# First layer of a four-layer kernel: scores as one 64-row product per head, projections of eight heads laid out through HBM

## Chip, cores and metric

The kernel runs on one core of one Trainium2 chip. The metric is the device time of the whole program in microseconds (us), the median of the runs. Engines are named as in the profile: PE (TensorE matmul), PEld (its weight load), DVE (VectorE), ACT (ScalarE), POOL (GpSimd), SP (SyncE, which here only issues DMAs).

## Reference

Four layers work one after the other on x (8 batches x 256 channels x 512 positions), with ctx of the same shape. The change touches the first one alone:

```python
q = Wq @ x + bq ; k = Wk @ ctx + bk ; v = Wv @ ctx + bv      # per batch, 256 x 512
# 16 heads of 16 channels each
attn = softmax((q * scale)^T k, masked keys -> -inf)         # per head 512 x 512
mean = attn @ v ; ex2 = attn @ (v * v)                       # per head 512 x 16
std  = sqrt(relu(ex2 - mean * mean))
out  = (instance_norm(x, mask) * std + mean) * mask
```

Layers 2 (a recurrent block), 3 (two cross attentions and an MLP) and 4 (a non-local block) are the same code before and after.

## The kernel before

**Precision.** PE multiplies float32 operands of the kind fp32r in one pass, at less than full precision. So every operand A is kept as a high part (A rounded) and a low part (A minus high), and a product is high x high + high x low + low x high: three passes that accumulate in the same PSUM bank.

**Heads and groups.** `layer0` handles the 16 heads of a batch in four groups (`G0`) of four heads (`HG`); there are 8 batches, so 32 groups. A head has 16 channels, but gets 32 rows of the 128 partitions: 16 for the channels, row `ROW_MASK` for the additive mask of the keys (the queries hold 4.0 there), row `ROW_MAX` for the negated maximum of the query (the keys hold 1.0 there). The tiles QH, QL (queries, high and low) and KH, KL (keys) have 128 partitions = 4 heads x 32 rows, a slot for each of the four groups, and 512 columns. `project_queries` (6 passes of 512 columns) and `project_keys` (6 passes and one with MSELR that adds the mask row) make them for one group. ACT evicts the PSUM bank as the high part (L545, L550), DVE then evicts the same bank as the low part (L684, L689).

**A group** is 8 steps (`NT`; n = 0 to 7), each for one pair of heads and one quarter of the 512 keys. In a step PE does, in this order: `scores` (L417: three passes, each for two heads in two different 32-row parts of the array, into two of the four banks BT), `maxima` (L394: one high x high pass for the group two ahead, into the two banks BM), `weighted` of the step before (L431: exponentials times values and squares, for two heads), and then what else that step carries. ACT takes the exponential of the score banks (L582), DVE the maximum over the maxima banks (L695). Further work in a step: n = 1 `turn_maxima` (a transpose, which DVE casts to NMT), n = 2 and 6 `turn_pair` (four transposes of the result, of which DVE takes the moments), n = 3 `project_queries` and n = 4 `project_keys` for the group three ahead, in group 3 n = 5 and 7 `values` of the next batch, in group 2 n = 7 `statistics`.

**What sets the order.** It is written out by hand: each engine has its own program, and semaphores join them. `maxima(n)` waits until DVE has read `maxima(n-1)` (one pair of banks BM), `scores(n)` waits for the exponential of n - 2, `weighted(n)` for that of n, `weighted` of a group's first step also for the squares that ACT writes (`square_values`, L567). SP places the four turned maxima of a group as one row each by DMA (`place_maxima`, L177), a group before they are used; scores of a group wait for them. ACT's square roots in group 0 (`roots`) need other tables: a load before them and one behind. Ahead of the first group (the prologue) PE projects three groups and DVE takes the maxima of two groups, 16 reductions.

Of the kernel before, what the change touches and what calls it, by code (L numbers as in the profile page):

```python
# [5 lines left out]

# [14 lines left out]
G0 = 4  # L21
HG = H0 // G0
CG = HG * D0
ROW_MASK, ROW_MAX = D0, D0 + 1
# [3 lines left out]
NEG = -1e30  # L28
# [21 lines left out]
def layer0(nc, x, xT, ctx, mask_row, mask_col, wqk, qkb, aug, wv, bv, mask_sel, ident_in, x1T):  # L50
# [5 lines left out]
    with ExitStack() as stack:  # L56
# [17 lines left out]
        WH = sb("wh", [P, G0, LC, 2, P], F32R)  # L74
        WL = sb("wl", [P, G0, LC, 2, P], F32R)
        WVH = sb("wvh", [P, LC, L], F32R)
        WVL = sb("wvl", [P, LC, L], F32R)
        QKB = sb("qkb", [P, 2, G0])
        AUG = sb("aug", [P, 2, G0])
        BVB = sb("bvb", [P, L])  # L80
        MSEL = sb("msel", [P, P])
        MSELR = sb("mselr", [P, P], F32R)
# [16 lines left out]
        QH = sb("qh", [P, G0, E], F32R)  # L99
        QL = sb("ql", [P, G0, E], F32R)  # L100
        KH = sb("kh", [P, G0, E], F32R)
        KL = sb("kl", [P, G0, E], F32R)
# [15 lines left out]
        WQK = EX[:, 0:2, :, :].rearrange("p n a (b c d) -> p (n a) b c d", b=LC, c=2)  # L118
# [3 lines left out]

        consts_in, inputs_in, stats_x_in, memset_done, inputs_read, mask_read, stats_read = [sem(n) for n in ("consts_in", "inputs_in", "stats_x_in", "memset_done", "inputs_read", "mask_read", "stats_read")]
# [23 lines left out]
        def head_rows(p, a):  # L147

            h = 2 * p + a
            return slice(32 * h, 32 * h + 32)  # L150

        @block.sync
        def _(sp):
# [17 lines left out]
            def place_maxima(b, g):  # L171
# [4 lines left out]
                for h in range(HG):  # L176
                    sp.dma_start(QH[32 * h + ROW_MAX:32 * h + ROW_MAX + 1, g, :].bitcast(F32),  # L177
                                 NMT[h * EC:(h + 1) * EC, g % 2, :].bitcast(F32)).then_inc(max_in, 16)
# [3 lines left out]
            for dst, src in ((QKB[:, :, :], qkb), (AUG[:, :, :], aug), (MSEL[:, :], mask_sel), (WV, wv), (BVB[:, :], bv),  # L182
                             (ID[:, :], ident_in)):
                sp.dma_start(dst, src).then_inc(consts_in, 16)
            load_statistics(0)
            place_maxima(0, 0)
            load_inputs(1)
            place_maxima(0, 1)
            with sp.Fori(0, B - 2) as b:
# [3031 lines left out]
```

## Time and profile before

| | us |
|---|---|
| median of 3 runs | 4405.9 (4405.7 to 4408.11) |
| span of the profiled execution | 4404.7 |
| PE busy over the span | 4165.1 (95%) |
| DVE busy | 2982.4 (68%) |
| ACT busy | 1964.2 (45%) |
| POOL busy | 1591.1 (36%) |
| mean granted TensorE clock | 0.978 |
| HBM read, written | 220.27 MB, 15.73 MB |

The profiled execution stands 1.2 us below the median. The chain of waits that the page prints covers the last layer alone; for the first layer the timeline is what tells. The first layer runs from 0 to about 829 us.

### The profile page before, as it was taken

How to read it: one execution, taken by the hardware profiler on the slowest of the kernel's cores; microseconds unless marked ns; L12 is line 12 of the kernel's file. 1: busy time of each engine (PE TensorE's matmuls, PEld its weight loads, DVE VectorE, ACT ScalarE, POOL GpSimd, SP SyncE). 2: the span in 40 equal slices, each digit the busy share in tenths (PEclk: the TensorE clock that was granted, in tenths of full speed). 3: DMA queues.
4: the chain of work that ended last, by engine and by line, in shares of the span. 5: the costliest groups of instructions: out<-in, count | busy, mean ns of one | idle time of the engine just before them, and what ended most of it. 6: DMA issues, size and time to landing. Idle time of an engine off the chain costs nothing. (4 is left out here: it accounts for less than half of the span.)

```text
span 4404.7 us, 70578 instructions
## 1 busy us (share of the span) xinstructions
PE 4165.1 (95%) x22060; PEld 3143.8 (71%) x22060; DVE 2982.4 (68%) x6501; ACT 1964.2 (45%) x3814; POOL 1591.1 (36%) x1094
## 2 busy tenths in 40 slices
PE   7999999778999997799999999999999999999999
PEld 3444444356777775588887797887887877988866
DVE  5666666268888887475775775767766757757743
ACT  2555555322333331355553455553555543555522
POOL 1223233145566563133234323234332234332230
PEclk7999999889999999899999999999999999999999
DMA  1000000300000000222112322222222122231122
GB/s 40 26 20 30 20 20 11 125 5 11 15 15 15 16 10 15 90 63 83 58 60 74 103 63 73 64 72 72 92 65 71 58 70 99 63 96 56 54 78 98
DMA packets 128413, 239.26 MB, mean 54 GB/s; under 512 B 16933, under 2 KB 40101, under 8 KB 126897
## 3 DMA queue, kind: packets, MB, share of 16 engines
q1 hardware_dynamic: 126544, 232.46, 16.5%
q0 software_dynamic: 1008, 3.67, 0.2%
q8 instruction: 123, 2.02, 0.2%
q14 instruction: 114, 0.93, 0.1%
q10 hardware_dynamic: 624, 0.18, 0.0%
HBM read 220.27 MB, written 15.73 MB: 54 GB/s over the span
## 5 line engine op out<-in xcount | busy, mean ns | idle before, releaser
L2105 POOL TENSOR_TENSOR c_wl<-c_wr,c_wh 128x512 fp32r<-128x512 f32 (+1 forms) x576 | 822.0, 1439 | 1646.0 <-ACT c_wh L2472 1388.7
L2573 ACT ACTIVATE c_pr<-c_ps,c_nms 128x257 f32<-128x257 f32 x512 | 244.2, 477 | 485.1 <-DVE c_nms L2795 483.1
L582 ACT ACTIVATE a_ex<-a_ps 128x1024 f32<-128x1024 f32 x256 | 261.1, 1023 | 259.7 <-PE a_ps L417 259.7
L1629 DVE TENSOR_TENSOR_SCAN b_sb<-b_wt,b_s,b_ps 128x256 f32<-128x256 f32 x512 | 361.6, 735 | 15.6 <-PE b_ps L1082 3.2
L695 DVE TENSOR_REDUCE a_nm<-a_ps 128x2 f32<-128x1024 f32 x256 | 311.4, 1221 | 80.5 <-PE a_ps L394 80.3
L2472 ACT ACTIVATE c_wh<-c_wr 128x512 fp32r<-128x512 f32 (+1 forms) x464 | 315.3, 687 | 45.4 <-PE c_ps L2192 41.6
L1580 POOL TENSOR_TENSOR b_sb<-b_sb,b_rt 128x1024 f32<-128x1024 f32 x128 | 277.9, 2178 | 156.5 <-DVE b_sb L1629 113.9
L2190 PE MATMUL c_ps<-c_hh,c_wh 128*128 128x512 f32 x768 | 309.1, 402 | 12.9 <-DVE c_hl L2679 12.6
L2190 PE MATMUL c_ps<-c_gh,c_wh 128*128 128x512 f32 x768 | 307.7, 401 | 5.6 <-DVE c_gl L2857 2.9
L2192 PE MATMUL c_ps<-c_hh,c_wl 128*128 128x512 f32 x768 | 304.4, 396 | 0.0
L2191 PE MATMUL c_ps<-c_hl,c_wh 128*128 128x512 f32 x768 | 303.8, 396 | 0.0
L2190 PE MATMUL c_ps<-c_wh,c_cth 128*128 128x256 f32 x1024 | 303.5, 296 | 0.0
L2192 PE MATMUL c_ps<-c_gh,c_wl 128*128 128x512 f32 x768 | 303.3, 395 | 0.0
L2191 PE MATMUL c_ps<-c_gl,c_wh 128*128 128x512 f32 x768 | 302.9, 394 | 0.0
L2192 PE MATMUL c_ps<-c_wh,c_ctl 128*128 128x256 f32 x1024 | 288.3, 282 | 0.0
L2191 PE MATMUL c_ps<-c_wl,c_cth 128*128 128x256 f32 x1024 | 287.7, 281 | 0.0
L431 PE MATMUL a_ps<-a_ex,a_vf 128*64 128x512 f32 x1024 | 278.9, 623 | 8.9 <-ACT a_ex L582 7.9
L2793 DVE TENSOR_REDUCE c_nm<-c_ps 128x1 f32<-128x257 f32 x512 | 214.9, 420 | 69.5 <-PE c_ps L2192 69.3
L1094 PE MATMUL b_ps<-b_xf,b_w 128*128 128x256 f32 x1056 | 243.6, 384 | 12.1 <-DVEq L1688 10.1
L1094 PEld LDWEIGHTS b_ps<-b_xf,b_w 128*128 128x128 f32 x1056 | 199.9, 192 | 46.3 <-issue 14.7
L2837 DVE TENSOR_TENSOR c_gl<-c_g,c_gh 128x512 fp32r<-128x512 f32 x128 | 89.2, 702 | 206.1 <-ACT c_gh L2555 206.1
L2789 DVE TENSOR_SCALAR c_pr<-c_pr,c_rs 128x257 f32<-128x257 f32 x512 | 196.1, 383 | 40.3 <-issue 1.0
(379 smaller groups left out, 10578.6 us busy)
## 6 DMA issues: line engine op xcount, KB each, us to landing
c_wr<-in_downs SPq DMA_DIRECT2D x192, 256.0 KB, 2.7
c_wr<-in_wv SPq DMA_DIRECT2D x64, 512.0 KB, 3.9
c_wr<-in_wk SPq DMA_DIRECT2D x128, 256.0 KB, 2.9
c_wr<-in_wq SPq DMA_DIRECT2D x128, 256.0 KB, 2.6
c_wr<-in_fc SPq DMA_DIRECT2D x64, 256.0 KB, 2.8
b_w<-in_w SPq DMA_DIRECT2D x8, 1024.0 KB, 14.7
a_x<-in_x SPq DMA_DIRECT2D x8, 512.0 KB, 3.9
a_ctx<-in_ctx SPq DMA_DIRECT2D x8, 512.0 KB, 4.4
```

The costliest lines, as they stand in the source:

```text
L431: mm = pe.matmul(ps[64 * a:64 * a + VCOLS, BO, :], VF[:, k, g * HG + 2 * p + a, :], EX[:, n % 4, a, :], start=(k == 0), stop=(k == EC - 1) ...
L582: act.activation(EX[:, n % 4, :, :], ps[:, BT + 2 * (n % 2):BT + 2 * (n % 2) + 2, :], ACT.Exp).then_inc(ex_ready, 1)
L695: dve.tensor_reduce(NM[:, s, :].rearrange("p (h c) -> p h c", h=HG)[:, 2 * p:2 * p + 2, c:c + 1], ps[:, bank:bank + 2, :], AX.X, ALU.max, ...
L1094: mm = pe.matmul(half(bank, o), W[:, w, k, o * P:(o + 1) * P], src[:, k, :], start=(k == 0), stop=(k == EC - 1), skip_group_check=True)
L1580: pool.tensor_tensor(SB[:, quad % RING, :, :, 0:L], SB[:, quad % RING, :, :, 0:L], RT[:, third(b, q // 8)].unsqueeze(1).broadcast_to([P, 2 ...
L1629: mm = dve.tensor_tensor_scan(SB[:, quad % RING, pr % 2, e, 1:L + 1], WT[:, third(b, i), e, :], half(spread_bank(pair), e), S0[:, b % 2, 2 ...
L2105: pool.tensor_tensor(piece(WL, slot), piece(WR, slot), piece(WH, slot), ALU.subtract).then_inc(piece_cut[slot], 1)
L2190: pe.matmul(out, sh, mh, start=start, stop=False, skip_group_check=True)
L2191: pe.matmul(out, sh, ml, start=False, stop=False, skip_group_check=True)
L2192: return pe.matmul(out, sl, mh, start=False, stop=stop, skip_group_check=True)
L2472: act.activation(piece(WH, slot), piece(WR, slot), ACT.Copy).then_inc(piece_high[slot], 1)
L2573: act.activation(PR[:, i, 0:L + 1], ps[:, BS + 1 - i % 2, 0:L + 1], ACT.Exp, bias=NMS[:, i:i + 1], scale=float(K2) ** -0.5, accum_out=RS[: ...
```

## The change

- A head has 64 rows: 16 with the high part, 16 that pair high with low, 16 that pair low with high, the mask row (48, `ROW_MASK`) and the row of the maximum (49, `ROW_MAX`); rows 50 to 63 hold zeros. Queries hold high, high, low, and keys hold high, low, high. So one pass is the whole score. `scores` has one pass in place of three; `maxima` stays one pass, now with all 64 rows.
- The projections yield eight heads of 16 rows without gaps (an "oct", `OCT` = 2 for each batch) in place of four heads of 32. There are two of each kind in a batch in place of four, in groups 0 and 2, and for the next batch. The pass with MSELR is gone; the mask row is written by DMA.
- The 64-row layout is made by DMA: SP writes the high and low parts to a tensor `strips` in HBM (7 writes for an oct: `write_queries`, `write_keys`) and reads them back into the tiles QP and KP (4 reads for a group: `place_strips`), once the scores that read the slot are done. Constant rows are written to HBM at the start by four DMAs of ACT.
- The rounding of ctx to its high part (`cut_c` on ACT) moves from group 1, n = 0 to group 0, n = 0, ahead of the squares of the values; that of x (`cut_x`) to group 3, n = 5. `mask_rows` and `count_valid` on DVE move from groups 0 and 1 to group 3.
- In the prologue the four projections of batch 0 go to four banks in one go, then the values, then the maxima of two groups.

```diff
-ROW_MASK, ROW_MAX = D0, D0 + 1
+ROWS = 64
+ROW_MASK, ROW_MAX = 3 * D0, 3 * D0 + 1
+OCT = 2
...
+            def write_queries(b, o):
+
+                for g in (2 * o, 2 * o + 1):
+                    sp.wait_ge(strips_in[g], b * N_STRIPS + AHEAD)
+                    sp.sem_inc(passed, 1)
+                sp.wait_ge(qh_ready, b * OCT + o + 1 + AHEAD)
+                sp.sem_inc(passed, 1)
+                sp.dma_start(scratch_rows(0, o, 0, D0), QH[:, :].bitcast(F32)).then_inc(scratch_in[o], 16)
+                sp.dma_start(scratch_rows(0, o, D0, D0), QH[:, :].bitcast(F32)).then_inc(scratch_in[o], 16)
+                sp.wait_ge(ql_ready, b * OCT + o + 1 + AHEAD)
+                sp.sem_inc(passed, 1)
+                sp.dma_start(scratch_rows(0, o, 2 * D0, D0), QL[:, :].bitcast(F32)).then_inc(scratch_in[o], 16)
...
+            def place_strips(b, g):
+
+                sp.wait_ge(scratch_in[g // 2], (b + 1) * N_SCRATCH + AHEAD)
+                sp.sem_inc(passed, 1)
+                sp.wait_ge(t_ps, (b * G0 + g - G0 + 1) * NT + AHEAD)
+                sp.sem_inc(passed, 1)
+                for s, tile in ((0, QP), (1, KP)):
+                    for a in range(2):
+                        heads = strips[s, g // 2, :, HG * (g % 2) + a:HG * (g % 2) + HG:2, :]
+                        sp.dma_start(tile[head_rows(a), g, :, :].bitcast(F32), heads).then_inc(strips_in[g], 16)
...
             with sp.Fori(0, B - 2) as b:
-                place_maxima(b, 2)
+                place_strips(b + 1, 1)
                 place_maxima(b, 3)
                 load_statistics(b + 1)
+                load_inputs(b + 2)
+                write_queries(b + 1, 1)
+                write_keys(b + 1, 1)
+                place_strips(b + 1, 2)
                 place_maxima(b + 1, 0)
-                load_inputs(b + 2)
+                place_strips(b + 1, 3)
                 place_maxima(b + 1, 1)
+                write_queries(b + 2, 0)
+                write_keys(b + 2, 0)
+                place_strips(b + 2, 0)
+                place_maxima(b + 1, 2)
...
-                pe.matmul(ps[:, BX, :], MSELR[:, :], MBRR[:, :], start=False, stop=True).then_inc(k_ps, 1)
...
-                for i, (keys, queries) in enumerate(((KH, QH), (KH, QL), (KL, QH))):
-                    for a in range(2):
-                        rows = head_rows(p, a)
-                        mm = pe.matmul(ps[:, BT + 2 * (n % 2) + a, :], keys[rows, g, cols], queries[rows, g, :], start=(i == 0), stop=(i == 2))
+                for a in range(2):
+                    rows = head_rows(a)
+                    mm = pe.matmul(ps[:, BT + 2 * (n % 2) + a, :], KP[rows, g, p, cols], QP[rows, g, p, :], start=True, stop=True)
...
-                    if left > 2 and n == QUERIES_AT:
+                    if projected and n == QUERIES_AT:
...
-                        project_queries(*after(b, g, 3))
-                    if left > 2 and n == KEYS_AT:
-                        project_keys(*after(b, g, 3))
+                        project_queries(b + 1, g // 2)
+                    if projected and n == KEYS_AT:
+                        project_keys(b + 1, g // 2)
...
-                    if g == 1 and left > 2 and n == 0:
+                    if g == 0 and more and n == 0:
                         cut_c(b + 1)
```

PE in step n = 4 of a group that projects, before (a_qh, a_ql, a_kh and a_kl are the tiles of queries and keys, a_ch and a_cl ctx, a_ps PSUM):

```order
L417 MATMUL a_ps<-a_qh,a_kh 128x512 [waits a_ex_ready]
L417 MATMUL a_ps<-a_qh,a_kh 128x512
L417 MATMUL a_ps<-a_ql,a_kh 128x512 x2
L417 MATMUL a_ps<-a_qh,a_kl 128x512 x2
L391 REGISTER_ALU
L394 MATMUL a_ps<-a_kh,a_qh 128x512 [waits a_m_read]
L394 MATMUL a_ps<-a_kh,a_qh 128x512
L431 MATMUL a_ps<-a_ex,a_vf 64x512 [waits a_ex_ready]
L431 MATMUL a_ps<-a_ex,a_vf 64x512
L352 REGISTER_ALU [waits a_mask_ready,a_c_low]
L355 MATMUL a_ps<-a_ch,a_wh 128x512 [waits a_ql_ready,a_qh_ready]
```

And the same step after (a_qp and a_kp are the 64-row tiles):

```order
L481 MATMUL a_ps<-a_qp,a_kp 128x512 [waits a_ex_ready]
L481 MATMUL a_ps<-a_qp,a_kp 128x512
L461 MATMUL a_ps<-a_kp,a_qp 128x512 [waits a_m_read]
L461 MATMUL a_ps<-a_kp,a_qp 128x512
L495 MATMUL a_ps<-a_ex,a_vf 64x512 [waits a_ex_ready]
L495 MATMUL a_ps<-a_ex,a_vf 64x512
L423 MATMUL a_ps<-a_ch,a_wh 128x512 [waits a_ql_ready,a_qh_ready]
```

Four of the eight row-tiled matmuls are gone, and the wait for a_m_read (DVE has read the maxima before) stands two passes nearer to the step's start.

ACT at the start of group 0 in the loop before (a_ex the exponentials, a_ot the result of a pair, a_vf values and squares):

```order
L582 ACTIVATE a_ex<-a_ps 128x1024 [waits a_w_ps]
L572 ISA
L573 REGISTER_ALU [waits a_w_ps]
L574 ACTIVATE a_ot<-a_ps 128x512 [waits a_tr_ps]
L565 ISA
L566 ISA [waits a_vs_ready]
L567 ACTIVATE a_vf<-a_vs 128x4x4x16 [waits a_w_ps]
```

And after:

```order
L652 ACTIVATE a_ex<-a_ps 128x1024 [waits a_w_ps]
L642 ISA
L643 REGISTER_ALU [waits a_w_ps]
L644 ACTIVATE a_ot<-a_ps 128x512 [waits a_tr_ps]
L630 ACTIVATE a_ch<-a_ctx 128x1024 [waits a_v_ps,a_k_ps,a_inputs_in]
L636 ISA [waits a_vs_ready]
L637 ACTIVATE a_vf<-a_vs 128x4x4x16 [waits a_w_ps]
```

The rounding of ctx (128x1024) now stands ahead of the squares.

SP from step 3 of group 2 to step 1 of group 3 in the loop after (before, SP issued in this place the turned maxima and the loads of inputs, nothing else):

```order
L197 DMA strips<-a_qh 8x16x512
L200 DMA strips<-a_ql 8x16x512 [waits a_ql_ready]
L208 DMA strips<-a_kh 8x16x512 [waits a_mask_ready,a_kh_ready]
L209 DMA strips<-a_kh 8x16x512
L210 DMA strips<-a_mbrr 8x512
L213 DMA strips<-a_kl 8x16x512 [waits a_kl_ready]
L219 ISA [waits a_scratch_in1]
L224 DMA a_qp<-strips 64x2x512 [waits a_t_ps]
L224 DMA a_qp<-strips 64x2x512
L224 DMA a_kp<-strips 64x2x512 x2
L183 REGISTER_ALU
L187 DMA a_qp<-a_nmT 1x4x128 [waits a_nmT_sb]
```

The placing of the maxima now stands behind reads that wait for the end of a group's scores (a_t_ps).

## Rows read from the trace of the kernel before

**Rows 1.** Windows: busy us of PE, PEld, DVE, ACT, POOL; clock, DMA share, GB/s

```profile
0.00:60.00 60.00, 31.37 (x96) 19.72 (x96) 33.79 (x39) 8.88 (x11) 5.34 (x11) 0.73 0.22 73
258.00:350.00 92.00, 90.73 (x490) 44.26 (x488) 57.10 (x77) 49.86 (x59) 29.41 (x29) 1.00 0.08 24
```

**Rows 2.** Timeline, one plain step (start us, us, engine, line)

```profile
298.95 0.49 PE L417 MATMUL a_ps<-a_qh,a_kh 32*128 32x512 f32 x2
...
299.52 0.39 PE L417 MATMUL a_ps<-a_qh,a_kl 32*128 32x512 f32 x2
...
299.75 0.39 PE L394 MATMUL a_ps<-a_kh,a_qh 32*128 32x512 f32 x2
...
299.96 1.02 ACT L582 ACTIVATE a_ex<-a_ps 128x1024 f32<-128x1024 f32 x1 [1.69 <-PE a_ps L417]
...
300.08 1.08 PE L431 MATMUL a_ps<-a_ex,a_vf 128*64 128x512 f32 x4
300.19 1.23 DVE L695 TENSOR_REDUCE a_nm<-a_ps 128x2 f32<-128x1024 f32 x1 [0.42 <-PE a_ps L394]
...
301.09 0.50 PE L417 MATMUL a_ps<-a_qh,a_kh 32*128 32x512 f32 x2
```

**Rows 3.** Timeline of the prologue and the first scores

```profile
27.95 0.96 PE L394 MATMUL a_ps<-a_kh,a_qh 32*128 32x512 f32 x6
...
29.44 3.48 DVE L695 TENSOR_REDUCE a_nm<-a_ps 128x2 f32<-128x1024 f32 x3
...
31.84 0.80 PE L394 MATMUL a_ps<-a_kh,a_qh 32*128 32x512 f32 x2 [0.63 <-DVE a_nm L695]
...
60.27 0.79 PE L417 MATMUL a_ps<-a_qh,a_kh 32*128 32x512 f32 x2 [2.89 <-DVE a_nm L695]
```

**Rows 4.** Timeline, projections in steps 3 and 4 of a group

```profile
265.48 0.50 PE L341 MATMUL a_ps<-a_xh,a_wh 128*128 128x512 f32 x1
...
267.06 0.50 PE L417 MATMUL a_ps<-a_qh,a_kh 32*128 32x512 f32 x2
...
269.21 0.50 PE L355 MATMUL a_ps<-a_ch,a_wh 128*128 128x512 f32 x1
...
271.04 0.50 PE L417 MATMUL a_ps<-a_qh,a_kh 32*128 32x512 f32 x2
...
271.15 0.69 ACT L550 ACTIVATE a_kh<-a_ps,a_qkb 128x512 fp32r<-128x512 f32 x1 [1.15 <-PE a_ps L358]
...
271.87 0.75 DVE L689 SCALAR_TENSOR_TENSOR a_kl<-a_ps,a_qkb,a_kh 128x512 fp32r<-128x512 f32 x1 [2.09 <-ACT a_kh L550]
```

**Rows 5.** Timeline, ACT's extra work in groups 0 and 1, and who waits

```profile
258.74 0.41 ACT L567 ACTIVATE a_vf<-a_vs 128x256 f32<-128x256 f32 x1
...
259.39 0.65 PE L431 MATMUL a_ps<-a_ex,a_vf 128*64 128x512 f32 x2
...
273.10 1.28 ACT L612 ACT_TABLE_LOAD   x1
...
277.16 1.94 ACT L582 ACTIVATE a_ex<-a_ps 128x1024 f32<-128x1024 f32 x2
...
278.24 1.08 PE L431 MATMUL a_ps<-a_ex,a_vf 128*64 128x512 f32 x4 [1.13 <-ACT a_ex L582]
...
282.16 1.05 ACT L560 ACTIVATE a_ch<-a_ctx 128x1024 fp32r<-128x1024 f32 x1
```

**Rows 6.** Timeline, DVE's extra work beside the reductions

```profile
279.82 0.95 DVE L799 RECIPROCAL a_st<-a_st 128x128 f32<-128x128 f32 x1
...
329.02 0.41 DVE L748 TENSOR_TENSOR a_st<-a_st 128x256 f32<-128x256 f32 x1
...
330.24 0.15 DVE L753 RECIPROCAL a_rn<-a_nv 128x1 f32<-128x1 f32 x1
```

**Rows 7.** DMA issues: size, us to landing; and SP's issues of one group

```profile
c_wr<-in_downs SPq DMA_DIRECT2D x192, 256.0 KB, 2.7
...
261.19 2.49 SPq L177 DMA_DIRECT2D a_qh<-a_nmT  x4
```

More of the change, by code:

```diff
@@ L7 @@
+import itertools
 from contextlib import ExitStack
@@ L279, in group_0 @@
                 copy_values(b, 1)
+                if more:
+                    cut_c(b + 1)
                 if prior is not None:
@@ L443, in before, with group @@
                 return (b, g - 1) if g > 0 else (b - 1, G0 - 1)
-            def group(b, g, left=3, first=False):
+            def group(b, g, left=3, first=False, more=True):
                 it = b * G0 + g
+                projected = more and g % 2 == 0
                 for n in range(NT):
@@ L574, in take_pair, with group @@
                 act.activation(OT[:, p, :], ps[:, BO, :], ACT.Copy).then_inc(ot_ready, 1)
-            def group(b, g, left=3, prior=None, first=False, more=True):
+            def group(b, g, prior=None, first=False, more=True, further=True):
                 it = b * G0 + g
@@ L591, in group @@
                         square_values(b, g + 1)
[L592 to L593 removed]
+                    if more and g % 2 == 0 and n == QUERIES_AT:
+                        queries(b + 1, g // 2)
                     if n == 4:
                         take_pair(b, g, 0)
[L596 to L597 removed]
+                    if more and g % 2 == 0 and n == KEYS_AT:
+                        keys(b + 1, g // 2)
                     if g == 2 and n == 5:
@@ L620, in _ @@
             act.wait_ge(weights_split, 2 + AHEAD)
-            for g in range(3):
-                queries(0, g)
-                keys(0, g)
+            queries(0, 0, BT)
+            keys(0, 0, BT + 1)
+            queries(0, 1, BT + 2)
+            keys(0, 1, BT + 3)
             square_values(0, 0)
+            cut_x(1)
             group(0, 0, first=True)
@@ L753, in spread_of_x, with group @@
                 dve.reciprocal(RN[:, :], NV[:, :])
-            def group(b, g, left=3, prior=None, first=False, more=True):
+            def group(b, g, left=3, prior=None, first=False, more=True, further=True):
                 for n in range(NT):
@@ L767, in group @@
                             take_moments(b - 1, G0 - 1, 1)
-                    if left > 2 and n == QUERIES_AT:
-                        queries(*after(b, g, 3))
-                    if left > 2 and n == KEYS_AT:
-                        keys(*after(b, g, 3))
+                    if more and g % 2 == 0 and n == QUERIES_AT:
+                        queries(b + 1, g // 2)
+                    if more and g % 2 == 0 and n == KEYS_AT:
+                        keys(b + 1, g // 2)
                     if left and g == G0 - 1 and n == VALUES_AT[0]:
@@ L830, in _ @@
             mask_rows(0, 1)
+            queries(0, 0, BT)
+            keys(0, 0, BT + 1)
             count_valid(0)
```

311 lines of the change are left out of this document (165 added, 146 removed).

## The prediction

> **What bounds the kernel now.** I read the windows first. In the middle of the first layer PE is busy 90.7 of 92 us at full clock, while DVE has 57.1, ACT 49.9 and POOL 29.4 [rows 1]. The change touches only this layer, which ends near 829 of 4404.7 us; the rest is left as it is.
>
> Next comes the timeline of a plain step [rows 2]. PE starts the first score pass at 298.95, the third at 299.52, the maxima pass at 299.75, the weighted product at 300.08, and the next step's scores at 301.09. So the step takes 2.14 us, without a gap. A pass costs 0.23 (299.52 to 299.75); a first pass after another shape costs 0.10 more (0.57 for two). ACT's exponential starts 0.44 behind the last score pass and takes 1.02. DVE's maximum starts 0.44 behind the maxima pass and takes 1.23. Both have room in 2.14 us. PE is the bound, so PE time removed is time won, until the next engine is met.
>
> **What is removed.**
> - Scores: 256 steps (32 groups x 8) lose two passes of 0.23 each. The saving is 256 x 0.46 = 117.8 us. The plain step becomes 1.68.
> - Projections: queries take 265.48 to 267.06 = 1.58, keys 269.21 to 271.04 = 1.83 with the mask pass [rows 4]. 29 of the 32 groups are projected inside steps, 29 x 3.41 = 98.9. After, there are 7 batches x 2, each 1.58 + 1.60, together 44.5. The saving is 54.4.
> - Prologue: scores start at 60.27 and the first maxima pass at 27.95, 32.3 us for 16 reductions. These alone need 16 x 1.16 = 18.6 (3.48 for three, [rows 3]); the rest is the third projection and the values, which now lie ahead of them. The first maxima must now wait for the layout: two projections to about 17 us, evictions of 0.69 and 0.75 [rows 4], seven writes at 0.62 per issue (2.49 for four) and 2.7 to land, four reads at the same prices [rows 7]. That comes to about 28 us, where the first maxima are today. I take 28 + 18.6 + 0.6 = 47, a saving of 13.
>
> Together 117.8 + 54.4 + 13 = 185 us.
>
> **What is given back**, where a shorter PE step uncovers another engine.
> - DVE's floor. There is one pair of maxima banks. The maxima pass, 0.44 to the reduction, 1.23 for it, and 0.12 until PE goes on (the second reduction ends at 29.44 + 2 x 1.14 = 31.72, PE starts at 31.84 [rows 3]) make 1.79 per step. Against 1.68 this costs 0.1 in the some 9 steps of a batch without PE extras: 7 us in all.
> - Behind the projection of keys. ACT starts 0.11 behind the step's first pass and takes 0.69; DVE's low part starts 0.03 later and takes 0.75; only then comes the reduction of 1.23, and 0.12 [rows 4, 2]. So the next maxima pass cannot start before 2.95 us into the step. Before, PE reached it at 2.14 + 0.80 = 2.94; now it is there at 2.0. Cost 0.95, in group 2 of seven batches and group 0 of the first: 8 x 0.95 = 7.6. Queries cost nothing: the keys' projection covers their eviction.
> - ACT in group 0. `cut_c` (1.05, [rows 5]) now stands ahead of the squares, for which the weighted product of step 1 waits. Before, the squares ended at 259.15 and PE went on at 259.39, a stall of 0.2 us. Now they come 1.05 - 0.46 = 0.6 later and PE is 2 x 0.46 = 0.9 earlier: 1.5 us more, in six batches, 9 us.
> - The square roots of group 0: the exponential of step 5, a table load at 273.10, two roots, a load, the exponential of step 6 at 277.16 and PE at 278.24 [rows 5], which waited 1.13. This chain hangs on step 5's start and is not shortened, so the three last steps stay at 8.0 us (before 8.2) and their saved 1.4 is lost but for 0.2: 1.2 x 7 = 8.5.
> - DVE's extra work. A reciprocal of 0.95 stands behind group 1's first reduction (2.3 us with it, against a step of 1.79), and 1.37 (329.02 to 330.39) ahead of the second in group 3 [rows 6]. Similar pieces lie at the seam of groups 1 and 2. I estimate 2 us per batch, 14 in all.
> - HBM layout, SP and its queue: nothing. An oct's strips are projected at steps 3 and 4 of a group. They are read at the end of that group or of a later one, and used a group after that, 15 us or more later. A read needs 4 x 0.62 + 2.7 = 5.2 [rows 7]. SP issues some 51 DMAs per batch of 80 us, 32 us. The turned maxima come behind the reads in SP's program but are ready only at step 1, when the reads (2.5 us of issue) are nearly out, and have over 10 us. Should a group be shorter than this path, all of the excess would show.
>
> Sum: 7 + 7.6 + 9 + 8.5 + 14 = 46. Net gain 185 - 46 = 139. Against the profiled span this gives 4404.7 - 139 = 4265.7; the median is 1.2 above the span, so 4267. A batch takes some 96 us now (60 to 829 us in eight) and should take about 81.
>
> **Two unknown prices.** No row shows a 64-row pass. It is bounded by the 32-row pair at 0.23, where both heads run at once, and by the two heads one after the other, 0.46. I take 0.23, the nearest row: it too has two heads in separate rows of the array.
>
> The Trainium skill ("TensorEngine Tiling (Array Packing)", Tiling Modes) lists two tiles of 64 rows x 128 columns that work in parallel, which is the first of these prices. The trace shows it for 32 rows only. By its sentence on mode switches, which drain the engine, nothing changes, since there are two switches per step before and after.
>
> The other is the write to HBM in 8 x 16 x 512 form, between the 2.7 us of a 256 KB load and twice that. In the loop either is hidden. In the prologue the double would take back some 5 of the 13 us.
>
> A rule that speaks against the layout: the Trainium skill ("DMA: Bandwidth & Descriptors", Why a DMA increments its semaphore by 16 and not by 1) says that a copy runs on the largest number of DMA engines up to 16 that divides the slowest dimension of both sides. That is 8 for the 8 x 16 x 512 side, half the engines. By this the doubled price would hold, and the time would be 4272 instead of 4267.
>
> **The rivals.**
> 1. The 64-row heads do not run at once. Each of the two row-tiled passes then costs 0.46, and the plain step stays at 2.14. The score saving is gone, and of the give-backs only ACT's squares stay: 54.4 + 13 - 9 = 58, so 4347. For it: no row has this shape. Against it: 32-row pairs do. Chance 0.06.
> 2. The give-backs are mostly hidden, for instance because the work overlaps more finely than my step by step count: up to 4405.9 - 185 = 4221. Against it: each is a chain read from rows. Chance 0.06 for below 4240.
> 3. Slower: the layout path becomes the bound. `maxima` for a group two ahead wait for strips that SP may read only once the old slot's scores are done. In group 0 the write and the two round trips then set the pace of every group. It decides once the reads land later than a group (15 to 16 us) after their issue, and the kernel is slower from about 16 + 139 / 28 = 21 us on. A landing of 25 us would give 28 x 9 - 139 = 113 us more, 4519. For it: SP is in order and strips move 7.3 MB per batch, some 90 GB/s on top of 24 [rows 1]. Against it: a 256 KB load lands in 2.7. Chance 0.03.
> 4. The clock. It was 0.73 in the first 60 us, where PE was busy 31.4 us and waited for DVE, and 1.00 where it was busy throughout [rows 1]. After, PE is busy some 73 of 80 us, with gaps of up to 1.5 us. If a tenth of the eight batches (65 us) ran at 1.2 in place of 2.4 GHz, it would cost 0.9 x 65 = 58 us: 4325. Chance 0.05.
>
> **The numbers.** My case has 0.80, with 4250 to 4290 as its own range. The range for all reaches down to 4235, halfway to the case without give-backs, and up to 4320, towards the clock and to late strips of a few us. That leaves out rival 1 (0.06), rival 3 (0.03), half of rivals 2 and 4, and some 0.04 beyond. A difference under 0.2% (9 us) cannot be told from none. Faster by more than that: 0.80 + 0.06 + 0.06 + 0.04 = 0.96, cut to 0.95. Same 0.01, slower 0.04.
>
> **What would show it.** The score pair should stand 0.34 ahead of the maxima pass, with plain steps of 1.7 to 1.8 us and DVE the releaser of the maxima pass. The step behind a keys' projection should be near 3.2 us, `weighted` in step 1 of group 0 should wait for ACT, and first scores should start near 47 us. PE waiting for DMA within a batch would prove me wrong, as would a score pair of 0.46, or a granted clock below 0.95 between 150 and 600 us.

## The result: 4275.6 us, and the profile after

The changed kernel takes 4275.63 us (median of 4 runs, 4275.28 to 4276.14), the kernel before 4406.14 us in the same session (4 runs, 4405.7 to 4408.11). The ratio is 0.970, with an interval of 0.969 to 0.972: faster by 130.5 us, where 139 were forecast. The profiled execution spans 4274.3 us, 130.4 less than before.

The windows of the trace come first. Columns are as in [rows 1]: length, busy us of PE, PEld, DVE, ACT and POOL, granted clock, DMA share, GB/s.

```profile
0.00:28.00 28.00, 8.18 (x24) 6.20 (x24) 8.20 (x12) 5.30 (x6) 4.59 (x9) 0.94 0.49 169
28.00:46.00 18.00, 8.36 (x41) 5.98 (x41) 12.87 (x14) 1.68 (x3) 0.40 (x1) 0.69 0.71 202
46.00:60.00 14.00, 6.65 (x21) 2.94 (x23) 9.42 (x9) 1.06 (x1) 2.69 (x2) 0.50 1.04 263
150.00:600.00 450.00, 420.38 (x1981) 170.52 (x1980) 307.63 (x413) 265.73 (x311) 168.77 (x174) 1.00 0.41 120
```

In the loop (last row) PE is busy 93% of the time at full clock, where [rows 1] has 99% (of another stretch). What is missing is the give-back: PE now waits for other engines. The DMA share has gone from 0.08 to 0.41. The first three rows are the prologue, and the DMA engines are full in the third.

A plain step and two that are held show how PE's time is spent. These are lines of the timeline of the changed kernel (start, length, engine, line, and in brackets how long the engine sat idle and what ended it). L481 is the score pair, L461 the maxima pass, L495 the weighted product, L763 DVE's reduction, L652 the exponential. The rows from 314.07 answer to [rows 2], and with the key eviction at 314.90 to [rows 4].

```profile
314.07 0.50 PE L481 MATMUL a_ps<-a_qp,a_kp 64*128 64x512 f32 x2
...
314.41 0.39 PE L461 MATMUL a_ps<-a_kp,a_qp 64*128 64x512 f32 x2
...
314.90 0.75 DVE L757 SCALAR_TENSOR_TENSOR a_kl<-a_ps,a_qkb,a_kh 128x512 fp32r<-128x512 f32 x1 [1.41 <-ACT a_kh L617]
...
315.57 1.22 DVE L763 TENSOR_REDUCE a_nm<-a_ps 128x2 f32<-128x1024 f32 x1
...
315.75 0.49 PE L481 MATMUL a_ps<-a_qp,a_kp 64*128 64x512 f32 x2
...
316.84 0.51 PE L461 MATMUL a_ps<-a_kp,a_qp 64*128 64x512 f32 x2 [0.60 <-DVE a_nm L763]
...
318.87 0.50 PE L481 MATMUL a_ps<-a_qp,a_kp 64*128 64x512 f32 x2
...
320.94 1.08 PE L495 MATMUL a_ps<-a_ex,a_vf 128*64 128x512 f32 x4 [1.33 <-ACT a_ex L652]
...
321.95 0.50 PE L481 MATMUL a_ps<-a_qp,a_kp 64*128 64x512 f32 x2
```

From 314.07 to 315.75 is one step of PE's own work: 1.68 us, as forecast. The score pair stands 0.34 ahead of the maxima pass, so a 64-row pair costs what a 32-row pair does. The next step lasts 3.12 (to 318.87), because DVE evicted `a_kl` before it reduced. The last lasts 3.08, because the exponential stands behind two square roots and two table loads. Counted in this way, a batch in the middle takes 21.87 + 15.42 + 23.77 + 19.51 = 80.57 us (groups 0 to 3), where it was 95.8 and some 81 were forecast.

Who made PE wait between 80 and 600 us, by the view of waits (us in total, times, longest):

```profile
PE a_ps L461 <- DVE a_nm L763: 15.7, 32, 0.9
PE a_ps L495 <- ACT a_vf L637: 8.4, 6, 1.4
PE a_ps L495 <- ACT a_ex L652: 8.0, 6, 1.3
```

These three are the give-backs that the prediction lists, and there is none for a DMA. The view counts idle time alone: the step at 315.75 lasts 3.12 us, where a step of this kind with three passes (below) takes 2.72 and should take 2.26 with one. That is 0.86 more, and the view shows a wait of 0.60. So a give-back is better read from the length of steps than from this view.

The prologue is where the forecast failed. The timeline of the changed kernel there, which answers to [rows 3] (L196 to L213 are SP's writes to the strips, L224 its reads):

```profile
16.43 0.76 SPq L196 DMA_DIRECT2D strips<-a_qh  x1
...
20.40 1.68 SPq L210 DMA_DIRECT2D strips<-a_mbrr  x1
...
22.20 1.06 SPq L213 DMA_DIRECT2D strips<-a_kl  x1
...
28.04 0.69 ACT L613 ACTIVATE a_qh<-a_ps,a_qkb 128x512 fp32r<-128x512 f32 x1 [9.31 <-DMA strips<-a_kl]
28.17 1.32 SPq L224 DMA_DIRECT2D a_qp<-strips  x2
...
35.95 0.97 PE L461 MATMUL a_ps<-a_kp,a_qp 64*128 64x512 f32 x6
...
48.83 1.65 PE L461 MATMUL a_ps<-a_kp,a_qp 64*128 64x512 f32 x6 [2.46 <-DMA a_kp<-strips]
...
59.34 0.79 PE L481 MATMUL a_ps<-a_qp,a_kp 64*128 64x512 f32 x2 [3.07 <-DVE a_nm L763]
```

SP issues the seven writes from 16.43 to 23.26, they have landed at 28.04, the first maxima start at 35.95 and the first scores at 59.34. The forecast had 47, and before it was 60.27. So the 13 us of the prologue came out as 0.9, and that is 12 us less than forecast.

Where the rest of the 130.4 lies is seen at PE's first matmul of layer 2, which starts at 833.00 us before and at 707.43 after. So the first layer is 125.6 us shorter, 0.9 of it in the prologue and 124.7 behind it, where 126 were forecast. The other 4.8 us lie in layers 2 to 4, whose code is the same. From that matmul to the end, the kernel before and its variant with one pass take 3571.7 and 3572.6 us, the changed kernel and its nine variants 3564.1 to 3567.9. No run asks for the cause, and it stays open.

### The profile page after: what moved, and what is told of

It reads as the page before. It is cut to its first block and busy times, and to the rows that moved or that the text cites. A ratio compares the mean times of both kernels' runs of the same rounds, so it can differ in the third digit from the quotient of the medians.

```text
span 4274.3 us, 68335 instructions
## 1 busy us (share of the span) xinstructions
PE 3998.9 (94%) x20812; PEld 3013.6 (71%) x20812; DVE 2939.8 (69%) x6467; ACT 1935.0 (45%) x3782; POOL 1592.7 (37%) x1094
## 5 line engine op out<-in xcount | busy, mean ns | idle before, releaser
L652 ACT ACTIVATE a_ex<-a_ps 128x1024 f32<-128x1024 f32 x256 | 260.9, 1022 | 212.8 <-PE a_ps L481 212.8
L763 DVE TENSOR_REDUCE a_nm<-a_ps 128x2 f32<-128x1024 f32 x256 | 311.5, 1221 | 60.7 <-PE a_ps L461 59.1
L495 PE MATMUL a_ps<-a_ex,a_vf 128*64 128x512 f32 x1024 | 278.1, 621 | 20.5 <-ACT a_ex L652 9.8
L1165 PE MATMUL b_ps<-b_xf,b_w 128*128 128x256 f32 x1056 | 243.6, 384 | 12.1 <-DVEq L1759 10.1
```

Of the source, the lines that this page charges most:

```text
L495: mm = pe.matmul(ps[64 * a:64 * a + VCOLS, BO, :], VF[:, k, g * HG + 2 * p + a, :], EX[:, n % 4, a, :], start=(k == 0), stop=(k == EC - 1) ...
L652: act.activation(EX[:, n % 4, :, :], ps[:, BT + 2 * (n % 2):BT + 2 * (n % 2) + 2, :], ACT.Exp).then_inc(ex_ready, 1)
L763: dve.tensor_reduce(NM[:, s, :].rearrange("p (h c) -> p h c", h=HG)[:, 2 * p:2 * p + 2, c:c + 1], ps[:, bank:bank + 2, :], AX.X, ALU.max, ...
L1165: mm = pe.matmul(half(bank, o), W[:, w, k, o * P:(o + 1) * P], src[:, k, :], start=(k == 0), stop=(k == EC - 1), skip_group_check=True)
```

## The experiments

Ten kernels were run. The kernel before, timed beside them, had 4406.5 to 4407.2 us.

### Each score pass three times

```diff
-                for a in range(2):
-                    rows = head_rows(a)
-                    mm = pe.matmul(ps[:, BT + 2 * (n % 2) + a, :], KP[rows, g, p, cols], QP[rows, g, p, :], start=True, stop=True)
+                for i in range(3):
+                    for a in range(2):
+                        rows = head_rows(a)
+                        mm = pe.matmul(ps[:, BT + 2 * (n % 2) + a, :], KP[rows, g, p, cols], QP[rows, g, p, :], start=True, stop=True)
```

This kernel is called three_passes further on.

> The changed kernel with each score pass of 64 rows issued three times into the same banks (the result is that of the last pass, so the scores are unchanged): 256 steps get two passes of 0.23 us back. Theory of the prediction (a score pass costs 0.23, and the shorter steps uncovered DVE and ACT at some 43 us in all, which hide again when the steps are long): +118 - 43 = +75, so 4351 us, plain steps of 2.14 us. Rival: nothing was uncovered and the passes are worth their full time: +118, 4393 us. Second rival: the two 64-row heads of a pass do not run at once; then the step grows by 4 x 0.23, over 4450 us.

Measured: 4348.22 us (4346.59 to 4348.85), ratio 0.987 (0.985 to 0.988). Two steps' first rows in its timeline (the triple score passes are L482):

```profile
343.31 0.96 PE L482 MATMUL a_ps<-a_qp,a_kp 64*128 64x512 f32 x6
...
344.11 0.40 PE L461 MATMUL a_ps<-a_kp,a_qp 64*128 64x512 f32 x2
...
345.45 0.96 PE L482 MATMUL a_ps<-a_qp,a_kp 64*128 64x512 f32 x6
```

Three pairs take 0.80 (343.31 to 344.11), one takes 0.34, so a pair costs 0.23; the step is 2.14 again, and the batch 89.55. Two pairs are worth 256 x 0.46 = 117.8 us of PE time, but only 4348.2 - 4275.6 = 72.6 of time. The other 45.2 are what a short step uncovers. The rest of the change is worth 4406.1 - 4348.2 = 58. It holds nothing of the prologue (the first scores of this kernel come at 60.23), some 5 us that lie behind the first layer, and a loss: here too PE waits 1.09 us for the squares behind `cut_c` (at 331.90), and that step takes 3.49 us. Rival 1, two heads one after the other, falls.

### The kernel before with the high by high pass alone

This leaves the two small products out of the scores, and with them the low parts.

```diff
-                for i, (keys, queries) in enumerate(((KH, QH), (KH, QL), (KL, QH))):
-                    for a in range(2):
-                        rows = head_rows(p, a)
-                        mm = pe.matmul(ps[:, BT + 2 * (n % 2) + a, :], keys[rows, g, cols], queries[rows, g, :], start=(i == 0), stop=(i == 2))
+                for a in range(2):
+                    rows = head_rows(p, a)
+                    mm = pe.matmul(ps[:, BT + 2 * (n % 2) + a, :], KH[rows, g, cols], QH[rows, g, :], start=True, stop=True)
```

> The kernel before with the first score pass alone (high x high; the two passes with a low part are left out, so the scores have less precision). It has neither the HBM layout nor fewer projections. Theory: -118 us of passes, and some 60 us given back (0.95 behind each of the 29 projections of keys = 27.5, DVE's floor 7, square roots 8.5, DVE's extra work 14, squares 3): about 4348 us. Rival: the passes alone are the whole gain, and the halved projections brought nothing: about 4276 us.

Measured: 4356.83 us (4349.54 to 4361.08), ratio 0.988 (0.986 to 0.990), 9 above the expectation. Its undisturbed batch takes 21.15 + 19.88 + 23.70 + 22.60 = 87.3 us, 8.5 less than before, and by eight of these the time would be about 4338. What lengthened it by the other 19 us is seen in a row of its timeline and two windows:

```profile
170.33 1.80 PE L430 MATMUL a_ps<-a_ex,a_vf 128*64 128x512 f32 x4 [1.34 <-ACT a_ex L581]
```

```profile
150.00:171.00 21.00, 18.61 (x87) 7.40 (x87) 14.12 (x18) 14.77 (x18) 5.65 (x7) 0.99 0.00 1
171.00:182.00 11.00, 11.00 (x31) 2.94 (x28) 7.12 (x8) 5.94 (x8) 8.34 (x4) 0.50 0.01 3
```

PE waited 1.34 us for the exponential behind the roots, and then ran at 1.2 GHz for 11 us although it was busy throughout. This happened in group 1 of five batches. In the four of them that lie within the loop that group took 23.9 to 26.3 us in place of 19.9. Rival 4 of the prediction is thus real. The changed kernel has the same wait (1.33 at 320.94) and a clock of 1.00 from 150 to 600 us; only in the last batch, behind a wait of 1.82 us at 638.74, did it run at 0.50 from 640 to 642. Why the clock falls behind one such wait and not behind another stays open.

### cut_c behind the squares

```diff
-                    if g == 0 and more and n == 0:
-                        cut_c(b + 1)
...
                     if g == 0 and n == 0 and not first:
                         square_values(b, 0)
+                    if g == 0 and more and n == 0:
+                        cut_c(b + 1)
```

> The changed kernel with cut_c behind square_values at group 0, n = 0 on ACT. Theory: the weighted product of step 1 waits for the squares, which come 1 us earlier; exponential 1 then comes just in time. 6 batches x 1.0 = -6 us: 4269.5 us, and step 1 of group 0 falls from 3.5 to 2.5 us. Rival: the wait only moves to the exponential of step 1 or to the low part of ctx that the projection of keys needs: within 1 us of 4275.6.

Measured: 4270.80 us (4268.22 to 4273.32), ratio 0.969 (0.967 to 0.971). The timeline of this kernel:

```profile
301.96 0.50 PE L481 MATMUL a_ps<-a_qp,a_kp 64*128 64x512 f32 x2
...
302.65 0.41 ACT L637 ACTIVATE a_vf<-a_vs 128x256 f32<-128x256 f32 x1
...
302.96 1.05 ACT L630 ACTIVATE a_ch<-a_ctx 128x1024 fp32r<-128x1024 f32 x1
...
303.30 1.08 PE L495 MATMUL a_ps<-a_ex,a_vf 128*64 128x512 f32 x4 [0.46 <-ACT a_vf L637]
```

PE's wait in step 1 of group 0 falls from 1.40 to 0.46 us and the step from 3.50 to 2.55, in each batch: 0.95 x 6 = 5.7, and 4.8 in the medians.

### The square roots without their tables

The two square roots in the loop are left out (Identity in their place), so the output is not normed as in the reference.

```diff
-                act.activation(ST[:, 3, :], ST[:, 2, :], ACT.Sqrt, bias=EPS[:, 0:1])
+                act.activation(ST[:, 3, :], ST[:, 2, :], ACT.Identity, bias=EPS[:, 0:1])
-                act.activation(VAR[:, :, :], VAR[:, :, :], ACT.Sqrt).then_inc(std_ready, 1)
+                act.activation(VAR[:, :, :], VAR[:, :, :], ACT.Identity).then_inc(std_ready, 1)
```

> The changed kernel with the two square roots that ScalarE takes for the norm in the loop left out (Identity in their place, so the output is another), which leaves out their table loads too. My theory: in each of the 7 batches group 0 has one step in which TensorE waits about 1.4 us because ScalarE's exponentials stand behind the roots and their tables; without it group 0 goes from 21.9 to about 20.5 us, and the time to about 4275.6 - 7 x 1.4 = 4266 us. Rival: ScalarE is late for other reasons by then (squares, cut_x), the wait only moves to the next step, and the time stays within 3 us of 4275.6.

Measured: 4267.51 us (4263.87 to 4270.32), ratio 0.968 (0.967 to 0.970). The wait for `a_ex` is gone. The last step of group 0 takes 1.67 in place of 3.08 and the group 20.46 in place of 21.87, but group 1 takes 15.92 in place of 15.42. So 0.9 us is won in each of six batches. In the last one, which has no projections, group 0 goes from 18.21 to 15.61 and group 1 from 16.38 to 15.94. That makes 6 x 0.9 + 3.0 = 8.4, and the medians differ by 8.1. Some 1.6 of the 3.0 are the fallen clock of the changed kernel's last batch: with the weights in the order of the strips (below) these two groups take 17.51 and 15.52 at full clock. So the roots themselves are worth nearer 7 us, and their term of 1.2 x 7 = 8.5 had the right place and about the right size.

### The keys' eviction one reduction later

```diff
-                    if more and g % 2 == 0 and n == KEYS_AT:
+                    if more and g % 2 == 0 and n == KEYS_AT + 1:
```

> The changed kernel with VectorE's eviction of the low part of the projected keys taken one reduction later (behind the reduction of the step after KEYS_AT). My theory: the step that follows the projection of keys is held by VectorE's maxima standing behind that eviction, so that step goes from 3.1 to about 2.3 us, once in each of groups 0 and 2 of a batch; at about 0.5 us for each of 14 the time is about 4275.6 - 7 = 4269 us. Rival: VectorE's queue is full there, the next maxima are late by the same amount one step on, and the time stays at 4275.6 within 2 us.

Measured: 4272.21 us (4270.66 to 4276.64), ratio 0.969 (0.968 to 0.971), 3.4 less than the changed kernel, between theory and rival. The timeline of this kernel in group 0:

```profile
318.01 0.50 PE L481 MATMUL a_ps<-a_qp,a_kp 64*128 64x512 f32 x2
...
318.26 0.74 DVE L757 SCALAR_TENSOR_TENSOR a_kl<-a_ps,a_qkb,a_kh 128x512 fp32r<-128x512 f32 x1
318.40 0.51 PE L461 MATMUL a_ps<-a_kp,a_qp 64*128 64x512 f32 x2
...
320.43 0.50 PE L481 MATMUL a_ps<-a_qp,a_kp 64*128 64x512 f32 x2
...
323.20 0.65 PE L495 MATMUL a_ps<-a_ex,a_vf 128*64 128x512 f32 x2 [2.05 <-ACT a_ex L652]
```

The held step falls from 3.12 to 2.42 in groups 0 and 2. In group 2 that is kept (23.77 to 23.05 us). In group 0 PE only arrives earlier at ACT's chain of roots and waits 2.05 there in place of 1.33, so the group stays at 21.87. The stall behind the keys is thus paid once a batch, as the prediction counted it (0.95 x 8; measured 0.71 x 8 = 5.7).

The median shows 3.4 of these 5.7. In batches 1, 2, 4 and 5 (counted from 0) of the profiled run, the slowest of the four, the mean granted clock was 0.76 over 7 us around the end of the wait of 2.05 (in batch 1 it was 0.50 from 161 to 164 us), and groups 0 and 1 together took 38.7 to 38.8 us. In batches 3 and 6 it stayed at 1.00, with 37.3. So a longer wait at the roots brings rival 4 back, at about 1.5 us a time.

### Every read of the strips twice

```diff
+        QD = sb("qd", [P, G0, PAIRS, E], F32R)
+        KD = sb("kd", [P, G0, PAIRS, E], F32R)
...
-        N_SCRATCH, N_STRIPS = 7 * 16, 4 * 16
+        N_SCRATCH, N_STRIPS = 7 * 16, 8 * 16
...
+                        sp.dma_start((QD, KD)[s][head_rows(a), g, :, :].bitcast(F32), heads).then_inc(strips_in[g], 16)
```

The unused reads count on the same semaphore, so PE waits for them as well.

> The changed kernel with every read of the laid-out heads from HBM issued a second time into tiles that nothing uses. My theory: in the loop the layout path has room, no engine waits there for a transfer, so the batches stay at 80.6 us; in the prologue the first maxima wait for the reads and their wait grows by 5 to 10 us, the time comes to about 4282 us. Rival (the layout path is near its bound): the reads end after the group that needs them, the batches grow by several us each, and the time passes 4300 us.

Measured: 4296.09 us (4294.69 to 4299.88), ratio 0.975 (0.974 to 0.977), 20.5 more than the changed kernel. A window, and the timeline of its prologue (scores are L484 here, maxima L464):

```profile
150.00:600.00 450.00, 419.98 (x1994) 171.54 (x1990) 305.80 (x409) 265.32 (x311) 175.16 (x177) 1.00 0.66 168
```

```profile
40.79 1.65 PE L464 MATMUL a_ps<-a_kp,a_qp 64*128 64x512 f32 x6 [4.17 <-DMA a_kd<-strips]
...
59.78 1.65 PE L464 MATMUL a_ps<-a_kp,a_qp 64*128 64x512 f32 x6 [8.45 <-DMA a_kd<-strips]
...
80.22 0.80 PE L484 MATMUL a_ps<-a_qp,a_kp 64*128 64x512 f32 x2 [13.00 <-issue]
```

In the loop the DMA share rises to 0.66 and the batches stay at 80.6 to 80.9 us: the layout costs next to nothing there, even at 1.6 times the load on the DMA engines, and rival 3 falls. All of the loss is in the prologue, where the first scores come at 80.22, 20.9 later. The expectation had 5 to 10 for that, at the first maxima. These come 4.8 us later (40.79), the second group's 11.0 (59.78). The last 9.9 us stand ahead of the scores, in a wait of 13.00 for which the profile names no releaser.

### Weights in the order of the strips, so that each write is one dimension of 128

```diff
-            return strips[s, o, first:first + count, :, :].rearrange("r h e -> h r e")
+            return strips[s, o, first:first + count, :, :].rearrange("r h e -> (r h) e")
...
-        return W.reshape(2,128,2,128).transpose(3,0,2,1)
+        return W.reshape(2,8,16,2,128).transpose(0,2,1,3,4).reshape(2,128,2,128).transpose(3,0,2,1)
```

The biases of queries and keys are reordered in the same way.

> The changed kernel with the weight columns ordered (row, head) in place of (head, row), so that the 128 partitions of QH, QL, KH, KL are written to HBM as one dimension of 128 instead of 8 x 16. Theory: the writes ran on half of the DMA engines (DMA share 0.5 while they alone are under way in the prologue), and now run on all: share near 0.9, the first eight heads land near 23 instead of 28 us, first scores near 51 instead of 59.3: -8 us, 4267.5 us; the batches in the loop unchanged at 80.6 us. Rival: SP's issues or the landing time, not the engines, bound the prologue: under 2 us gained.

Measured: 4267.72 us (4266.06 to 4270.72), ratio 0.969 (0.967 to 0.970), 7.9 less than the changed kernel. Its timeline:

```profile
16.38 0.33 SPq L196 DMA_DIRECT2D strips<-a_qh  x1
...
20.23 0.35 SPq L213 DMA_DIRECT2D strips<-a_kl  x1
22.31 0.69 ACT L613 ACTIVATE a_qh<-a_ps,a_qkb 128x512 fp32r<-128x512 f32 x1 [3.55 <-DMA strips<-a_kl]
22.45 1.34 SPq L224 DMA_DIRECT2D a_qp<-strips  x2
...
30.02 0.74 PE L461 MATMUL a_ps<-a_kp,a_qp 64*128 64x512 f32 x4
...
50.38 0.79 PE L481 MATMUL a_ps<-a_qp,a_kp 64*128 64x512 f32 x2 [2.63 <-DVE a_nm L763]
```

The DMA share from 0 to 60 us, in 40 slices of 1.5 us each and in tenths, of this kernel:

```profile
DMA  0799999000058950899999999999999998100000
```

and of the changed kernel, where the 13th to the 18th slice (18 to 27 us) are the writes:

```profile
DMA  0799989000004555540189955558999999999999
```

The same bytes, written as one dimension of 128 rows, take 0.32 to 0.43 us of SP's time each for the first oct in place of 0.57 to 1.06 (the 16 KB mask row, which took the 1.68 above, takes 0.41), use 0.8 to 0.9 of the DMA engines' time in place of 0.5, and have landed 5.7 us earlier (22.31 for 28.04). Of these, 2.7 us are the earlier end of SP's issues (20.58 for 23.26) and 3.0 the shorter time from there to the landing. The first scores are 8.96 us earlier and the time is shorter by 7.9. The groups in the loop take what they took.

### Staging tiles of its own for the second oct

```diff
+        STAGE = [(QH, QL, KH, KL), tuple(sb(n + "1", [P, E], F32R) for n in ("qh", "ql", "kh", "kl"))]
...
-            write_queries(0, 1)
-            write_keys(0, 1)
+            write_queries(0, 1, 1)
+            write_keys(0, 1, 1)
```

ScalarE's and VectorE's evictions of that oct go to the same new tiles and wait for no earlier write.

> The changed kernel with staging tiles of their own (QH, QL, KH, KL) for the second oct of the first batch, so that ScalarE and VectorE evict it without waiting 9.3 us for the first oct's writes to land. My theory: the writes themselves, on half of the DMA engines, set the first scores; SyncE still reads the first oct behind its writes and writes the second oct behind those reads, so the first scores stay at about 59.3 us and the time at 4275.6 within 3 us. Rival: the shared staging tile is the cause of the late prologue; then the first scores come about 9 us earlier and the time to about 4266 us.

Measured: 4275.43 us (4272.78 to 4277.12), ratio 0.970 (0.969 to 0.972), the first scores at 59.92. ACT's wait of 9.3 us for the landed writes is gone and nothing follows from it: the second oct's writes stand behind the reads in SP's order all the same.

### The fixed rows later

```diff
-            sp.wait_ge(fixed_in, 2 * OCT * 16)
             write_queries(0, 0)
+            sp.wait_ge(fixed_in, 2 * OCT * 16)
             write_keys(0, 0)
...
-            for s, o in itertools.product(range(2), range(OCT)):
-                act.dma_start(strips[s, o, ROW_MASK:, :, :].rearrange("r h e -> r (h e)"), fixed_rows[s]).then_inc(fixed_in, 16)
...
             cut_x(0)
+            for s, o in itertools.product(range(2), range(OCT)):
+                act.dma_start(strips[s, o, ROW_MASK:, :, :].rearrange("r h e -> r (h e)"), fixed_rows[s]).then_inc(fixed_in, 16)
```

> The changed kernel with the fixed rows of the strips (1 MB) written behind the first cut_x instead of at the start. My theory: the inputs land 1.3 us earlier, as in the kernel before, and all that follows in the prologue with them; the fixed rows then share the DMA engines with nothing that is waited for, so the first scores come at about 58.0 us and the time is 4274 us. Rival: the fixed rows collide with the write and the read of the heads there instead, the first scores stay at 59.3 us and nothing is gained.

Measured: 4274.93 us (4271.85 to 4278.06), ratio 0.970 (0.969 to 0.972). Its timeline:

```profile
14.49 0.76 SPq L196 DMA_DIRECT2D strips<-a_qh  x1
...
28.11 1.32 SPq L224 DMA_DIRECT2D a_qp<-strips  x2
```

The inputs land earlier and the first write is issued 1.9 us earlier, but the reads can start no sooner than before (28.11 for 28.17), and the first scores come at 60.71. The outcome is the rival's, but not its cause. The DMA share was 0.00 from 14 to 15 us, so the fixed rows had been moved before the first write of the heads began. What their new place costs is ACT's time: it issues them for 2.52 us from 8.24 on, `cut_c` starts at 10.88, the projection of keys waits 1.01 us for the low part of ctx, and the first write of keys is issued at 18.35, only 0.5 us earlier than before. Why the writes, all issued by 21.47 in place of 23.26, land no earlier stays open.

### Four edits together

The edits are those shown above: `cut_c` behind the squares, the weights in the order of the strips, the fixed rows later, and the keys' eviction one reduction later.

> Four edits together: the next batch's cut_c behind the squares, weights ordered by (row, head) so that each layout write is one dimension of 128, the fixed rows of the strips written only behind the first cut_x, and VectorE's eviction of the low part of keys one reduction later. My theory: the gains of places that lie apart add up: 5 (squares) + 8 (writes) + 1 (inputs earlier) + 6 (eviction), so about 4256 us. Rival: what one edit frees the other only hands on (the eviction above all), and the time is that of the first two alone, 4275.6 - 4.8 - 7.9 = 4263 us.

Measured: 4259.05 us (4258.65 to 4261.95, 5 runs), ratio 0.967 (0.965 to 0.968), 16.6 less than the changed kernel. That is less than the theory's 20 and more than the rival's 13. The first scores come at 50.91, so the fixed rows add nothing here either. In group 2 the keys' eviction gives its 0.7 us a batch. In group 0 it lengthens PE's wait for the roots (12.3 us in six waits, the longest 2.1, between 80 and 600 us) and group 0 takes 20.9 to 21.8 us. Behind four of these waits (batches 1, 4, 5 and 6) the clock fell again, to 0.76 to 0.80 in the mean of 7 us, and groups 0 and 1 took 37.6 to 37.9 us in place of 36.3: 5.6 us in all, more than what is missing to the theory. This is the fastest of all the kernels.

## Why the prediction was right, and where a term was wrong

The direction, the size and the bound were right: 4267 forecast, 4275.6 measured, within the main case's own range. In spans, 139 us were forecast: the prologue gave 12.1 less, the rest of the first layer 1.3 less, and layers 2 to 4 gave 4.8 that no term had. This last part is luck.

- **PE sets the step.** Right. The plain step is 1.67 to 1.68 us, and a 64-row pair costs 0.23, which was taken from the 32-row pair and was unknown before.
- **The score passes, 117.8, and what is given back, 46.** Right within some 5 us: three_passes puts the net at 72.6, hence the give-back of the passes at 45.2. It is not quite the same sum as the 46. The place of `cut_c` costs most of its part in three_passes too (3.49 for a step of 2.34, six times, some 6 us after the 0.2 of before), so like is to be compared with like as 45.2 and 40.
- **The projections, 54.4.** The rest of the change is worth 58 beside three passes. Less the 5 behind the first layer, and with the 6 that `cut_c` takes from it, that is some 59 for the projections. Right within 5.
- **The rivals.** None came true in the changed kernel: 4347 would need heads one after the other, 4221 give-backs hidden (45.2 of them show), 4519 a late layout in the loop, 4325 a tenth of the loop at half clock. The clock did fall once, in the last batch (some 1.6 us), and in four batches each with the keys' eviction later and with the four edits together.
- **Behind the keys, 7.6.** Right in place and count. The step took 3.12, and 2.41 with the eviction out of its way: 0.71 x 8 = 5.7 us, of which the median kept 3.4. In group 0 it hides in the roots' chain, as the experiment shows.
- **ACT's cut_c ahead of the squares, 9.** Right in place and size: the step takes 3.50, where it took 2.56 before and a step shorter by 0.46 would be 2.10, so 1.4 in each of six batches. With `cut_c` moved 0.46 of each wait stays, and 4.8 us come back.
- **The square roots, 8.5.** Right: the last three steps of group 0 take 7.88 us, where 8.0 was forecast (before 8.20), and the time is 8.1 us less without the roots and their tables, some 1.6 of it the fallen clock. The 8.0 us of waits in the view above are not this term, since PE waited there before the change too.
- **DVE's floor, 7, and its extra work, 14.** No run tests these two alone, but three_passes beside the changed kernel sizes them together. From 322 to 381 us of the changed kernel the view of waits names nothing but DVE for PE (four waits, 1.9 us). These are groups 1, 2 and 3. They take 18.49, 25.32 and 21.72 us with three passes; less 8 x 0.46 each, they would take 14.81, 21.64 and 18.04. In the changed kernel they take 15.42, 23.77 and 19.51, which gives back 0.6, 2.1 and 1.5. Without the step behind the keys (0.85) that is 3.4 us a batch, 24 us in seven where 21 were forecast. The floor is a little higher than the 1.79 worked out: such steps take 1.82 to 1.85. That all of this is DVE's is argued, since the view accounts for half of it.
- **HBM layout, SP and its queue in the loop, nothing.** Right. PE waits there for no transfer, and twice the reads cost at most 0.3 us in a batch.
- **The prologue, "28 + 18.6 + 0.6 = 47, a saving of 13".** This is the term that was mis-sized: it measured 0.9. Its 28 was too low by its own prices: 17 + 0.69 + 0.75 + 7 x 0.62 + 2.7 + 5.2 is 30.7, and it is 28 or so only if the first issues run beside the projection of keys. The table takes its three parts.

| us | forecast | changed kernel | one dimension of 128 |
|---|---|---|---|
| first writes landed | 28 - 5.2 = 22.8 | 28.04 | 22.31 |
| from there to the first maxima | 5.2 | 7.9 | 7.7 |
| from there to the first scores | 19.2 | 23.4 | 20.4 |
| first scores | 47 | 59.3 | 50.4 |

The first part is the writes, and so in the main is the third. I priced a write at 0.62 to issue and 2.7 to land, from a 256 KB load and a tiny copy [rows 7], and held the double only as a bound of 5 us. In fact one write of 8 x 16 x 512 took 0.57 to 1.06 to issue in the first oct and up to 1.62 in the second, that of the mask row 1.68, and the last write 4.8 from the end of its issue to its landing. And I counted it once, although the second oct goes the same way: its reads landed 2.46 us after PE was ready for them (48.83). With the writes in one dimension both parts fall to within 1.2 of the forecast, and the first scores regain 8.96 of the missing 12.3 us.

The trace has the DMA engines at a share of 0.5 during these writes and at 0.8 to 0.9 in the other form. So the rule of the Trainium skill ("DMA: Bandwidth & Descriptors", Why a DMA increments its semaphore by 16 and not by 1) agrees with the trace: 8 of 16 engines for the slowest dimension of 8 would be a share of 0.5, though no view shows the engines one by one. The time of 4272 that the prediction worked out with the doubled price was the nearer one. The cost of issuing stands beside it and comes from the runs alone.

The second part is in the main the reads: four of 256 KB in flight together. The time to land of all the reads in the prologue of the changed kernel, by the view of DMA issues from 0 to 60 us (KB each, median us):

```profile
a_qp<-strips SPq DMA_DIRECT2D x8, 256.0 KB, 6.6
a_kp<-strips SPq DMA_DIRECT2D x8, 256.0 KB, 7.7
```

For the four that the first maxima need, issued from 28 to 31 us, they are 4.2 and 5.1. In the loop they are 3.9 and 4.8, and the load in [rows 7] has 2.7. A price read from loads of a later layer was too low for these four reads together, by 2.4 us. Which share of this is the number in flight and which the form of the read, no run separates. The last 0.5 us or so of the 7.9 are not the reads: PE was still at the values, at a granted clock of 0.50 until past 34 us. With tiles of its own for the second oct the values lie earlier, and the first maxima start at 35.62, waiting for `a_kp`, in place of 35.95.

One explanation of the late prologue fell: the shared staging tile (no gain with tiles of its own). The fixed rows at the start delay the inputs by 1.9 us, but their move gave nothing; since it held up ACT, and with it the keys, it does not settle what they cost.

## What to carry to other kernels

When a pass is removed from an engine that is the bound, price the step that is left against each engine in it, group by group: of 118 us of TensorE time 73 came out as time, and the other 45 were found beforehand within some 5 us by reading each chain. When a layout goes through HBM, look at the form of the write as much as at its bytes: as 8 x 16 x 512 the writes ran at a DMA share of 0.5, and the six of 256 KB took 4.5 us of SyncE's time, where in one dimension of 128 it was 0.8 to 0.9 and 2.2 us. Latency counts where nothing runs ahead of it, in the prologue, and a gain that lands in front of a chain which is late anyway is handed on and not kept.

## What the runs showed of the hardware that I had not expected

- A write of 256 KB to the strips took 0.32 to 0.43 us of SyncE's time to issue as one dimension of rows by 512, and 0.57 to 1.06 us as 8 x 16 x 512 (first oct). With reads under way the first form took up to 0.96 (L208 at 26.92 in its trace) and the second up to 1.62 (L208 at 33.21).
- The granted clock of TensorE fell to 0.50 for 11 us behind a wait of 1.34 us, in a stretch in which the engine was busy 18.6 of 21 us, in the kernel before with one pass; in the changed kernel a wait of 1.33 us at the same place left it at 1.00, and one of 1.82 us in the last batch was followed by 0.50 from 640 to 642 us. With the keys' eviction one reduction later the wait there was 2.05 us, and the clock fell behind it in four of six batches (to 0.50 for 3 us in the first of these). In the first 60 us of the changed kernel the clock fell from 0.94 to 0.69 and 0.50 while PE waited for strips and reductions.
- Twice the reads, at a DMA share of 0.66 in place of 0.41, changed no group of batches 1 to 6 by more than 0.3 us.
